# Four context transfers move from the sync queue to ScalarE's, with bulk loads spread and masks written ahead, in a four-layer transformer kernel

## What is computed

```
h = layernorm(x)
for l in range(4):
    xn = ln1(h);  q, k, v = xn @ Wq.T + bq, xn @ Wk.T + bk, xn @ Wv.T + bv      # 16 heads of 8
    scores = (q @ k.T + rel_shift((q + u) @ r.T)) / sqrt(8), causal mask
    h = h + (softmax(scores) @ v) @ Wo.T + bo
    h = h + gelu(ln2(h) @ W1.T + b1) @ W2.T + b2                                # width 512
x = x + h
x = x + experts(layernorm(x))     # router, 4 of 16 experts of width 32, and a shared one of 256
```

## Time and profile before

| | us |
|---|---|
| median of 3 runs | 2257.51 (2255.7 to 2258.29) |
| the profiled execution, its own time | 2253.86 |
| its span, first to last instruction | 2252.0 |
| PE busy | 2160.7 (96%) |
| DVE busy | 1909.5 (85%) |
| ACT busy | 1796.4 (80%) |
| POOL busy | 1288.5 (57%) |

### The profile page before, as it was taken

How to read it: one execution, slowest core, us unless ns; L and a number is a source line. 1 busy time by engine, 2 the same in 40 slices (tenths; PEclk the granted TensorE clock), 3 DMA queues, 4 the chain that set the end, 5 groups by cost and what they waited for, 6 DMA issues and landing times. The chain is left out here.

```text
span 2252.0 us, 80791 instructions
## 1 busy us (share of the span) xinstructions
PE 2160.7 (96%) x30224; PEld 1885.2 (84%) x30224; DVE 1909.5 (85%) x4659; ACT 1796.4 (80%) x2661; POOL 1288.5 (57%) x2277
## 2 busy tenths in 40 slices
PE   4899999999999999999999999999999999979999
PEld 4788888888888888888888888888888888758888
DVE  6788899888888888888888888888887888579996
ACT  2688888888888888888888888888887888855453
POOL 4556556655555555655555555555554555366764
PEclk8899999999999999999999999999999999989999
DMA  4445434443344434433444434433444444123443
GB/s 135 125 120 137 124 107 113 112 112 108 107 114 110 116 107 112 114 109 106 111 113 114 111 108 111 114 106 108 111 114 117 110 115 113 53 65 93 110 115 82
DMA packets 279136, 246.79 MB, mean 110 GB/s; under 512 B 38752, under 2 KB 269280, under 8 KB 278752
## 3 DMA queue, kind: packets, MB, share of 16 engines
q1 hardware_dynamic: 278752, 241.63, 39.7%
HBM read 31.24 MB, written 4.72 MB: 16 GB/s over the span
## 5 line engine op out<-in xcount | busy, mean ns | idle before, releaser
L998 DVE TENSOR_REDUCE rowmax<-bank 128x4 f32<-128x1024 f32 (+1 forms) x768 | 916.7, 1220 | 154.6 <-PE bank L589 120.9
L815 ACT ACTIVATE probs<-bank 128x1024 f32<-128x1024 f32 x768 | 737.6, 1023 | 132.0 <-PE bank L656 130.9
L656 PE MATMUL bank<-qstack,kstack 64*128 64x128 f32 (+1 forms) x4096 | 422.1, 300 | 16.9 <-DMA qstack<-maxrows 16.4
L589 PE MATMUL bank<-kstack,qstack 62*128 62x256 f32 (+1 forms) x4096 | 418.7, 298 | 8.1 <-DMA qstack<-base_turned 7.5
L656 PEld LDWEIGHTS bank<-qstack,kstack 64*128 64x128 f32 x4096 | 318.2, 192 | 38.6 <-DMA qstack<-maxrows 19.3
L589 PEld LDWEIGHTS bank<-kstack,qstack 62*128 62x128 f32 x4096 | 316.4, 193 | 9.1 <-issue 8.2
L1162 POOL CAST xn1T_parts<-xn1T 128x256 fp32r<-128x256 f32 x128 | 50.7, 396 | 465.5 <-ACT xn1T L823 465.5
L732 PE MATMUL bank<-w,hidden 128*128 128x128 f32 x2048 | 284.6, 282 | 3.4 <-ACT hidden L863 2.8
L614 PE MATMUL bank<-maskT_half,pick_half 64*128 64x128 bf16 (+1 forms) x3072 | 273.6, 242 | 14.4 <-ACT probs L815 10.8
L679 PE MATMUL bank<-probs,v_pad 128*32 128x256 f32 x4096 | 271.0, 382 | 0.6 <-DVE v_tok L979 0.6
L732 PEld LDWEIGHTS bank<-w,hidden 128*128 128x128 f32 x2048 | 249.7, 192 | 17.5 <-ACT hidden L863 3.1
(11 more groups left out here) (147 smaller groups left out, 5000.7 us busy)
## 6 DMA issues: line engine op xcount, KB each, us to landing
qstack<-base SPq DMA_DIRECT2D x384, 128.0 KB, 2.5
kstack<-base SPq DMA_DIRECT2D x384, 128.0 KB, 2.5
qstack<-base_turned SPq DMA_DIRECT2D x384, 128.0 KB, 2.4
turn_x<-turn_c SPq DMA_DIRECT2D x512, 32.0 KB, 1.8
ctx_den<-ctxT_raw SPq DMA_DIRECT2D x256, 64.0 KB, 2.0
ctx_num<-ctxT_raw SPq DMA_DIRECT2D x256, 64.0 KB, 2.0
factors<-rows_kept SPq DMA_DIRECT2D x64, 256.0 KB, 4.9
qstack<-maxrows SPq DMA_DIRECT2D x256, 16.0 KB
```

The costliest lines, as they stand in the source:

```text
L589: last = pe.matmul(bank[:, b0 + b, i * wide:(i + 1) * wide], qstack[rows, r, p0 + i, t * 128:(t + 1) * 128], kstack[rows, r, p0 + i, 0:wid ...
L656: last = pe.matmul(bank[:, b0 + b, i * wide:(i + 1) * wide], kstack[rows, r, p0 + i, kt * 128:(kt + 1) * 128], qstack[rows, r, p0 + i, q0: ...
L815: act.activation(probs[:, k], bank[:, A_BANK[k]:A_BANK[k] + 2, :], ACT.Exp, scale=SCALE).then_inc(exp_done[k], 1)
L998: dve.tensor_reduce(rowmax[:, n % 2, t, :, p0:p0 + heads], bank[:, M_BANK[k]:M_BANK[k] + 2, :].rearrange("p b (h c) -> p b h c", h=heads), ...
```

## The change

The context's four DMAs are issued by ACT, directly behind its copy and ahead of exp round 5; SP's `context` is gone. x is loaded in 16 parts of two sequences, not in 9 of up to four; the bias rows and w_o of layers 1 to 3 come in slots 20 to 26, `w_in` in three parts in every other slot, and the load of w_1 for the next layer 8 slots later. Three waits for `w_rest_landed` are added at the first unit of layer 1. The rounds m 3, m 5, a 3 and a 4 write their masks ahead of the scores like the others, and the masks of a 0 come ahead of the scores of m 5. POOL's `split_w1` for the next layer stands late in slot n + 5, no longer first in slot n + 6.

```diff
-X_STARTS = (0, 2, 4, 8, 12, 16, 20, 24, 28)
+X_STARTS = tuple(range(0, B, 2))
...
             def loads_behind(s):
+                if s >= 1 and s % 2 == 1 and 3 + s // 2 < len(X_STARTS):
+                    rows_of_x(3 + s // 2)
                 if s == 2:
-                    sp.dma_start(b_o[:], on_all("bo")).then_inc(middle_landed, 16)
-                    sp.dma_start(w_o[:], a["w_o"].rearrange("l p n -> p l n")).then_inc(middle_landed, 16)
-                if s == 3:
+                    sp.dma_start(b_o[:, 0:1], on_all("bo", 0, 1)).then_inc(middle_landed, 16)
+                    sp.dma_start(w_o[:, 0], a["w_o"][0]).then_inc(middle_landed, 16)
                     sp.dma_start(w_1[:], a["w_1"][0]).then_inc(w1_landed, 16)
                 if s == 4:
-                    sp.dma_start(b_2[:], on_all("b2")).then_inc(later_landed, 16)
+                    sp.dma_start(b_2[:, 0:1], on_all("b2", 0, 1)).then_inc(later_landed, 16)
                     sp.dma_start(b_1[:], a["b_1"].rearrange("p (l c) -> p l c", l=LAYERS)).then_inc(later_landed, 16)
-                if s >= 5 and s % 2 == 1 and s // 2 - 2 < LAYERS:
-                    ly = s // 2 - 2
+                if s in (4, 6, 8, 10):
+                    ly = (4, 6, 8, 10).index(s)
...
-                if s >= 1 and s % 3 == 1 and 3 + s // 3 < len(X_STARTS):
-                    rows_of_x(3 + s // 3)
-                if s in (12, 14, 17):
-                    ly = 1 + (12, 14, 17).index(s)
+                if s in (12, 14, 18):
+                    ly = 1 + (12, 14, 18).index(s)
...
+                if s == 20:
+                    sp.dma_start(b_v[:, 1:], on_all("b_v", 1, LAYERS)).then_inc(w_rest_landed, 16)
+                if s == 22:
+                    sp.dma_start(w_o[:, 1:], a["w_o"].rearrange("l p n -> p l n")[:, 1:]).then_inc(w_rest_landed, 16)
...
-            def context(n):
-
-                sp.wait_ge(context_out, n + 1)
-                at_least(sp, ctxT_ready, n)
-                for g in range(2):
-                    sp.dma_start(ctx_den[64 * g:64 * g + 64], ctxT_raw[1:128:2, g]).then_inc(den_landed, 16)
-                at_least(sp, proj_done, n)
-                for g in range(2):
-                    sp.dma_start(ctx_num[64 * g:64 * g + 64], ctxT_raw[0:128:2, g]).then_inc(num_landed, 16)
...
-                if live(s - 4):
-                    context(s - 4)
...
-                if s == N - B // 2:
-                    experts_early()
+                if N - B // 2 <= s < N - B // 2 + 10 and s % 2 == 0:
+                    experts_early((s - N + B // 2) // 2)
...
-                if s > 0 and s % B == B // 2 and layer(s) + 1 < LAYERS:
+                if s > 0 and s % B == 3 * B // 4 and layer(s) + 1 < LAYERS:
...
                 if live(s - 4):
-                    a_bank(s - 4, 4)
-                    a_scores(s - 4, 4, masks_behind=True)
+                    a_masks(s - 4, 4)
+                if live(s - 4):
+                    a_scores(s - 4, 4)
...
                 if live(s - 1):
-                    m_bank(s - 1, 5)
-                    m_scores(s - 1, 5, masks_behind=True)
+                    m_masks(s - 1, 5)
                 if live(s - 3):
                     a_masks(s - 3, 0)
+                if live(s - 1):
+                    m_scores(s - 1, 5)
+                if live(s - 3):
                     a_scores(s - 3, 0)
...
                 act.copy(ctxT_raw[:].rearrange("p g c -> p (g c)"), bank[:, PV_BANK, :]).then_inc(context_out, 1)
+                act.wait_ge(context_out, n + 1)
+                at_least(act, ctxT_ready, n)
+                for g in range(2):
+                    act.dma_start(ctx_den[64 * g:64 * g + 64], ctxT_raw[1:128:2, g]).then_inc(den_landed, 16)
+                at_least(act, proj_done, n)
+                for g in range(2):
+                    act.dma_start(ctx_num[64 * g:64 * g + 64], ctxT_raw[0:128:2, g]).then_inc(num_landed, 16)
...
-                if live(s - 6) and (s - 6) % B == 0 and (s - 6) > 0:
-                    split_w1(layer(s - 6))
...
+                if live(s - 5) and (s - 5) % B == 0 and (s - 5) > 0:
+                    split_w1(layer(s - 5))
```

More of the change, by code:

```diff
@@ L80 @@
 GT = 4
-EX_DMAS = 5
+W_IN_PIECES = 3
+EX_DMAS = W_IN_PIECES + 4
 HIGH, LOW = 3.0e38, -3.0e38
@@ L365, in layers_program @@
         CONST_DMAS = 4
-        MIDDLE_DMAS, LATER_DMAS, REST_DMAS = 2, 3, 2 * (LAYERS - 1)
+        MIDDLE_DMAS, LATER_DMAS, REST_DMAS = 2, 3, 2 * (LAYERS - 1) + 4
         SLOTS = range(-LEAD, N + LAG)
@@ L399, in _ @@
             rows_of_x(1)
-            sp.dma_start(b_v[:], on_all("b_v")).then_inc(consts_landed, 16)
+            sp.dma_start(b_v[:, 0:1], on_all("b_v", 0, 1)).then_inc(consts_landed, 16)
             rows_of_x(2)
             def loads_behind(s):
+                if s >= 1 and s % 2 == 1 and 3 + s // 2 < len(X_STARTS):
+                    rows_of_x(3 + s // 2)
                 if s == 2:
-                    sp.dma_start(b_o[:], on_all("bo")).then_inc(middle_landed, 16)
-                    sp.dma_start(w_o[:], a["w_o"].rearrange("l p n -> p l n")).then_inc(middle_landed, 16)
-                if s == 3:
+                    sp.dma_start(b_o[:, 0:1], on_all("bo", 0, 1)).then_inc(middle_landed, 16)
+                    sp.dma_start(w_o[:, 0], a["w_o"][0]).then_inc(middle_landed, 16)
@@ new lines, in loads_behind @@
+                if s == 20:
+                    sp.dma_start(b_v[:, 1:], on_all("b_v", 1, LAYERS)).then_inc(w_rest_landed, 16)
+                if s == 22:
+                    sp.dma_start(w_o[:, 1:], a["w_o"].rearrange("l p n -> p l n")[:, 1:]).then_inc(w_rest_landed, 16)
+                if s == 24:
+                    sp.dma_start(b_o[:, 1:], on_all("bo", 1, LAYERS)).then_inc(w_rest_landed, 16)
+                if s == 26:
+                    sp.dma_start(b_2[:, 1:], on_all("b2", 1, LAYERS)).then_inc(w_rest_landed, 16)
@@ new lines, in experts_early @@
+            def experts_early(i):
+                if i < W_IN_PIECES:
+                    wide = 2 * GU // W_IN_PIECES
+                    sp.dma_start(ex.w_in[:, i * wide:(i + 1) * wide], a["w_in"][:, i * wide:(i + 1) * wide]
+                                 ).then_inc(ex.landed, 16)
+                elif i == W_IN_PIECES:
+                    sp.dma_start(ex.w_router[:], a["router"]).then_inc(ex.landed, 16)
+                    sp.dma_start(ex.bias_rows[:], a["correction"].rearrange("(o e) -> o e", o=1).broadcast_to([128, E])
+                                 ).then_inc(ex.landed, 16)
+                    sp.dma_start(ex.eye[:], a["c_eye"]).then_inc(ex.landed, 16)
+                else:
+                    sp.wait_ge(w1_split, 2 * LAYERS)
+                    sp.dma_start(w_1[:].rearrange("p (b t d) -> p b t d", b=GT // T, t=T), x_tiles[:, 0:GT // T]
+                                 ).then_inc(ex.landed, 16)
@@ L537, in values, with m_mask @@
                 last.then_inc(v_done, 1)
-            def m_mask(k, half, first=True):
+            def m_mask(k, half):
                 heads = 4 if k < 2 else 2
@@ L545, in m_mask, with m_masks @@
                     c = (0 if k < 2 else 128) + half * 64
[L546 to L550, removed]
+                    pe.matmul(v[:, :, c:c + 64], pick_half[rows, half], mask_half[rows, half, 0:heads],
+                              start=(half == 0), stop=True, skip_group_check=True)
+            def m_masks(n, k):
                 if k == 0:
@@ L574, in m_masks, with m_scores @@
                     m_mask(k, 1)
-            def m_scores(n, k, masks_behind=False):
+            def m_scores(n, k):
                 r, b0 = n % RING, M_BANK[k]
@@ L590, in m_scores @@
                                          qstack[rows, r, p0 + i, t * 128:(t + 1) * 128],
-                                         kstack[rows, r, p0 + i, 0:wide], start=(masks_behind and i == 0), stop=True,
+                                         kstack[rows, r, p0 + i, 0:wide], start=False, stop=True,
                                          skip_group_check=True)
-                if masks_behind:
-                    m_mask(k, 0, first=False)
-                    last = m_mask(k, 1, first=False)
                 last.then_inc(scores_done[k], 1)
@@ L605, in m1, with a_mask @@
                 last.then_inc(max_turned, 1)
-            def a_mask(k, half, first=True):
+            def a_mask(k, half):
                 heads = 2 if k % 3 < 2 else 4
@@ L613, in a_mask, with a_masks @@
                     c = half * 64
[L614 to L618, removed]
+                    pe.matmul(v[:, :, c:c + 64], pick_half[rows, 2 + half], maskT_half[rows, half, 0:heads],
+                              start=(half == 0), stop=True, skip_group_check=True)
+            def a_masks(n, k):
                 if k == 0:
@@ L641, in a_masks, with a_scores @@
                     a_mask(k, 1)
-            def a_scores(n, k, masks_behind=False):
+            def a_scores(n, k):
                 r, b0 = n % RING, A_BANK[k]
```

(16 more changed lines are left out.)

22 lines of the change are left out of this document (5 added, 17 removed).

## The result

The changed kernel takes 2550.67 us (median of 4, 2541.89 to 2564.74) against 2256.61 before: ratio 1.131, 95% interval 1.126 to 1.137. It is 294 us slower. The forecast was 2445, in a range of 2320 to 2720.

The account below looks back on a forecast made before the run. A loop of ACT and PE, both nearly full, was taken to bound the kernel. 2253.9 + 207 (issues on ACT) - 20 (bulk loads) = 2441, and + 4 for the median = 2445 us; range 2320 to 2720.

Parts of the forecast that it names:

- The loop of ACT and PE: ACT and PE, both nearly full, wait for each other each slot; four issues on ACT add 1.63 us a slot.
- the term of 207 us: 127 intervals between context copies, each 1.63 us longer because ACT's four issues delay exp 5.
- SP's relief: 2.45 us taken from SP gains nothing in quiet slots; its wait for base_turned grows from 1.3 to about 5 us.
- Rival A: Issues on ACT nearly free, under 0.16 us each, so only the bulk loads' gain acts: 2237 us; chance 0.10.
- Rival B: Issues of SP and ACT alternate, ACT's four take 4.9 us: +518, 2755 us; chance 0.17 including mixtures.
- rival C: PE's clock falls because PE now idles 1.5 us once a slot: +95 us, 2540 us; chance 0.05.
- quiet intervals up to slot 26 are within 0.5 us of each other: Sign expected in the trace: intervals between context copies nearly equal in quiet slots, with the clock at 1.00.
- Bulk loads: Smaller, spread loads give back 20 us of the 24 lost outside quiet slots; bounds 5 and 30.
- Masks ahead: On PE, four rounds write masks first, the same matmuls in another order: 0 us, bounds +-13 us.

Follow-up runs that it names:

- e1: The changed kernel with the context's four transfers back on SP, all else as changed: 2238.52 us, ratio 0.992 to the kernel before.
- e2: The kernel before with only the context's four transfers moved to ACT, behind its copy: 2552.84 us, ratio 1.131.
- e6: The changed kernel with only the two denominator transfers on ACT and the two numerator transfers back on SP: 2300.82 us, ratio 1.021.
- e5: The changed kernel with six more matmuls of zeros a slot in PE's gap, behind the scores of round a 3: 2473.51 us, ratio 1.098.
- e3: The kernel before with the bulk loads spread, the waits for them, and split_w1 moved; masks and context as before: 2237.37 us, ratio 0.992.
- e4: The kernel before with only the masks of rounds m 3, m 5, a 3 and a 4 ahead of the scores: 2253.13 us, ratio 0.998.
- e8: The kernel before with the bulk loads spread and the context's four transfers issued by POOL ahead of the split of xn1T: 2261.51 us, ratio 1.002.

## Why the prediction was right and where it was off

*The loop of ACT and PE.* Right, by e1, e2 and e6. The price of the four issues, taken from SP, was 2.45 us; they took 1.15 + 1.26 and a gap, 2.44. The slot was forecast at 16.4 us and is 16.48: the term of 207 us measured 216. The sum had exp 5 start at the end of the last issue, and it starts 0.11 us behind it. PE's gap ahead of down is 1.72 us for 1.5, the gap ahead of the slot's first exp is gone, the one ahead of L830 remained. One reading was off without effect: PE's slack is given as 0.06 to 0.3 us at three places, and by the prediction's own times it is 0.01 us at the third (1115.45 to 1115.46).

*SP's relief.* Worth nothing in a quiet slot, as forecast. SP's wait for base_turned, as the queue's own waits show, grew by what was taken from it and by the longer slot:

```profile
SPq L473 <- POOL base_turned L1187: 799.0, 127, 8.6
```

6.3 us a slot, not about 5, and 1.3 before. The Trainium skill (Perfetto Trace Analysis, DMA Optimizations) advises balancing over the DMA-capable engines where descriptor generation is the bottleneck, and names an engine that looks busy with it as the sign. Here the sign was there, but not the bottleneck: the full queue wasn't waited for, the receiving one was, and the move gave a loss.

*Rival A, free issues.* Refuted: 490 ns in the median for the denominators, 622 for the numerators.

*Rival B, two issuers in each other's way.* Not seen in the issues. 458 of ACT's 512 begin while an issue of SP is under way, and their medians are 496 ns (denominators) and 622 ns (numerators), against 484 and 620 for the others. SP's own issues of content have a median of 602 ns (qstack), against 600 before. The Trainium skill (Perfetto Trace Analysis, DMA Instruction — HWDGE) has the generator locked for exclusive use; if it is, no median of these rows shows a wait for the lock. What did grow is the time to landing, 3.0 and 3.2 us for content against 2.5; the prediction had no term for it, and what it costs in the changed kernel no run measures.

*The clock: the step that failed.* The prediction gave rival C 0.05 and put nothing into the sum, because PE would be busy 14.6 of 16.4 us, more than in a stretch of 15 us that had kept its full clock. That compared means over whole slots; the idle time is one gap of 1.7 us in each, and the lower level followed such gaps in part of the slots. e5 measures the clock term at 77 us. The price worked out for rival C was 95 us, but for another pattern, 0.75 us in each of 127 slots; the runs show about 1.6 us in most of 47 slots and nothing in the others, so that the two are near is luck, and its chance was too low. The sign "quiet intervals up to slot 26 are within 0.5 us of each other" failed with it: 12 of the first 26 intervals are more than 0.5 us above the quiet one.

*The range.* 2551 lies above the 2360 to 2520 us that had the chance of 0.62, in the stretch given to rival B, whose mechanism wasn't seen. That the stated range holds it is due to the room left for B, not to a term for the clock.

*Bulk loads.* 20 us back were forecast and e3 measures 19 alone; but in the changed kernel they bring 2. The terms were added as if independent, and they aren't. Why is not shown: it may be that where ACT holds the loop the waits saved on PE's side were already paid for, or that 18 of the 25 us before lie in four slots in which the clock fell as well, and in the changed kernel and e2 the clock falls in 47 and 48 slots anyway.

*Masks ahead.* 0 forecast, -3.5 us measured (e4), within the bounds.

Together: 2445 + 9 (slot) + 77 (clock) + 18 (bulk gain not realised) = 2549, measured 2551. That the sum closes is partly luck: each term comes from medians whose runs spread by 6 to 23 us, and some issues on ACT last long (denominators 490 ns in the median, 1750 at most; the gap behind the copy is over 3.1 us in 18 of 128 slots), which has no term.

## What to carry to other kernels

Before moving an issue to another queue, ask which queue is waited for: here a full queue with slack cost nothing, and 2.4 us on an engine that is full cost all but its gaps. If an issue must stand on a busy engine, put it behind an instruction whose result it doesn't need, one per instruction, and look after the transfer that becomes last. And when a change opens a gap on PE once per iteration, add a term for the clock.

## What the runs showed that was not expected

- ACT issues a DMA while its own ACTIVATE is still running: against e1's quiet slot of 14.72 us, four issues of 0.5 to 0.6 us cost 1.76 us behind the copy that they wait for, 1.51 in one block behind exp 5, and nothing when dealt out one behind each of four instructions.
- With gaps of the same size in two neighbouring slots (1.72 and 1.74 us), PE's clock fell in one and not in the other; in all it was at its lower level in 47 of the 127 intervals. Zeros multiplied by zeros in the gap, 1.24 us of them, kept it at its full level.
- An issue costs about the same on SP (0.58), ACT (0.49 to 0.62) and POOL (0.54 to 0.60 us). On SP and ACT single ones last up to 1.9 us, SP's with SP issuing alone as well; on POOL none of the 512 of e8 lasts over 0.78 us.
- Issues of ACT that begin during an issue of SP are no longer than others, but content and numerators land 0.5 to 1.2 us later in every run in which another queue than SP issues the numerators. Which of the two changes the landing, the queue or the time at which content is issued, no run separates.
